# A state-space vision layer on one core: low part, third time step and two products moved by one unit in the scan loop

## Chip, cores and metric

One core of a Trainium2 chip. The metric is the device time of the whole kernel in microseconds (us), lower is better. The kernel before took 372.35 us (median of 3 runs, 372.12 to 372.91).

## What is computed

A patch embedding, a selective state-space block (Mamba) and a mixture of experts, on 16 images of 64 tokens (1024 tokens), all in float32:

```python
h = patches @ proj_w.T + proj_b + pos_emb                 # 1024 x 192
# state-space block on layernorm(h); I = 384 channels, N = 16 states per channel
hidden, gate = split(layernorm(h) @ in_proj_w.T)
hid = silu(causal_conv(hidden, conv_w) + conv_b)          # 4 taps
ts, Bm, Cm = split(hid @ x_proj_w.T)                      # 48, 16 and 16 wide
dt = softplus(ts @ dt_proj_w.T + dt_proj_b)               # last token's times alpha
state[t] = exp(A * dt[t]) * state[t-1] + dt[t] * Bm[t] * hid[t]
y[t] = sum over states of state[t] * Cm[t]
h = h + ((y + hid * D) * silu(gate)) @ out_proj_w.T
# experts: 8, the best 2 of each token, and a shared one
h = h + sum_e cw[e] * ffn_e(layernorm(h)) + ffn_shared(layernorm(h))
```

## The kernel before

The tokens go in two groups g of 8 images (512 tokens), the 384 channels in three chunks i of 128 (one channel per partition). A vector z = 3g + i is one chunk of one group. The 16 states in halves of 8 and the 4 token tiles of a group make 8 slices of a vector, so there are 48 units n of 128 x 1024 elements: 0 to 23 for group 0 and 24 to 47 for group 1. Unit 24 is the first of vector 3, the "second group's first vector".

For each unit:

- ScalarE writes exp(A dt) into `decays`, four units (one k = n // 4) at a time (`decays_of(k)`, line 861). It waits until the products of the buffer's last use are done (`cs_ok`), and for the end of the time step's product (`end_ok`).
- TensorE makes the inputs dt B hid in PSUM (`inputs(n)`, line 1757) from `diagB` (B on block diagonals) and `stacked_u` (the transposed dt hid, copied so that it multiplies `diagB`). The PSUM banks alternate, so inputs(n) waits for scan n-2.
- VectorE scans (`scanned(n)`, line 1208) in place over `decays`.
- GpSimd multiplies by C (`weighted(n)`, line 623). TensorE sums over the states by transposing matmuls (`summed(n-3)`, line 1803).

Each engine has its own queue, written out by hand as a loop over the 48 units with `if n == ...` places for the other work; within a queue nothing overtakes. What group 1 needs before unit 24 runs so, i being the chunk:

- ScalarE makes the linear step and its logarithm (lines 794 to 802), which lands in `dt[1]` and `u` (`lnp_ok`).
- VectorE's `time_step(1, i)` (line 1145): dt = max(dt, 0) + u, all in SBUF.
- GpSimd's `inputs_of(pool, 1, i)` (lines 632 and 634): the last token's dt times alpha, then u = dt hid (`u_ok`).
- TensorE's `u_transposes(3)` in unit 21 (line 1666), into a PSUM bank.
- ScalarE's `u_high_part(3)` (line 837): the bank rounded to the format of TensorE's fast float32 path.
- VectorE's `u_low_part(3)` (line 1197): the bank less the high part.
- TensorE's `u_copies(3, half)` in units 22 and 23 (lines 1697 and 1699), which wait for both parts; ScalarE's `u_stacked(3, half)` (line 853) copies them to `stacked_u`. The first stands between the two halves of `decays_of(6)`, which belongs to units 24 to 27.

VectorE also builds the 8 slices of `diagB` for group 1 (`diagonal(1, s)`, line 1113) behind scans 18 to 25, and `segment_starts` clears the first column of each segment (line 1214, 0.11 us) behind scan 22 among others. The vectors 4 and 5 take their low part in another way, on ScalarE (`u_low_copy`). Their transposes stand in units 25 and 34.

The places in VectorE's and GpSimd's loop that the change touches are these; behind each `if` the steps stand in the order of the code.

Of the kernel before, what the change touches and what calls it, by code (L numbers as in the profile page):

```python
# [59 lines left out]
def program(nc, xT_d, projT_d, projb_d, pos_d, inT_d, par_d, xpT_d, dtT_d, outT_d, gateT_d, w13T_d, w2T_d, out_d):  # L60
    ctx = ExitStack()
    with ctx:
# [539 lines left out]
        def inverse_deviation(pool, chain, n):  # L602

            pool.wait_ge(aggr_ok, n + 1)
            sl = slice(TPG * (n % G), TPG * (n % G) + TPG)
            chain(pool.tensor_scalar(veps[:, sl], mv[:, sl, 1], EPS, 1.0, ALU.add, ALU.mult))
            if n != 1:
                pool.tensor_tensor(rstd[:, sl], veps[:, sl], neghalf[:, :], ALU.pow).then_inc(rstd_ok, 1)
                return
            pool.tensor_scalar(less_mean[:, :], mv[:, sl, 0], -1.0, None, ALU.mult)  # L610
            chain(pool.tensor_tensor(rstd[:, sl], veps[:, sl], neghalf[:, :], ALU.pow))
            pool.tensor_tensor(less_mean[:, :], less_mean[:, :], rstd[:, sl], ALU.mult).then_inc(rstd_ok, 1)

        def weighted(pool, n):

            g, i, s = of_unit(n)
            pool.wait_ge(scan_ok, n + 1)
            if i == 0 and s % 2 == 0:
                pool.wait_ge(c_ld[s // 2], 16 * (g + 1))
            if n >= SLOTS:  # L620
                pool.wait_ge(nsum_mm, n - SLOTS + 1)
            k, t = n // TPG, n % TPG
            pool.tensor_tensor(states[:, n % SLOTS, :].rearrange("p (n b s) -> p n b s", n=NH, b=2),  # L623
                               decays[:, k % DBUF, t, :, :, :].rearrange("p b n s -> p n b s"),
                               c_all[:, s, :].rearrange("p (n b s) -> p n b s", n=NH, b=2),
                               ALU.mult).then_inc(cs_ok, 1)

        def inputs_of(eng, g, i):

            eng.wait_ge(dt_ok, IC * g + i + 1)  # L630
            end = dt[g][:, i, S - 1::S]
            eng.tensor_tensor(end, end, par[:, i, P_ALPHA:P_ALPHA + 1].to_broadcast([128, GB]), ALU.mult).then_inc(end_ok, 1)
            eng.wait_ge(end_ok, IC * g + i + 1)
            eng.tensor_tensor(u[:, i, :], dt[g][:, i, :], hid[g][:, i, :], ALU.mult).then_inc(u_ok, 1)

        @block.gpsimd
        def _(pool):
# [39 lines left out]
            def diagonal_of(s):  # L677
                h, t = s // TPG, s % TPG
                pool.tensor_tensor(
                    diagB[:, s, :, :, :],  # L680
                    on_diagonal[:, :].unsqueeze(1).unsqueeze(1).to_broadcast([128, BLOCKS, NH, BLOCK]),
                    b_copied[:, :, t, NH * h:NH * (h + 1)].unsqueeze(3).to_broadcast([128, BLOCKS, NH, BLOCK]),
                    ALU.mult).then_inc(diag_pool, 1)
# [4 lines left out]
            for n in range(UNITS):  # L688
                weighted(pool, n)
                if n < 2:  # L690
                    diagonal_of(BUILT_BY_POOL[2 + n])
                if n == 2:
                    inputs_of(pool, 0, 1)
                if n == 6:
                    inputs_of(pool, 0, 2)
                if n in (18, 21, 23):
                    inputs_of(pool, 1, (18, 21, 23).index(n))
                if n == 44:
                    inverse_deviation(pool, chain, G)

# [320 lines left out]
        def _(dve):  # L1021
# [7 lines left out]
            def statistics(t, added):  # L1029
                dve.wait_ge(added, t + 1)  # L1030
                dve.bn_stats(stats[:, t, :], h0[:, t, :])
# [60 lines left out]
            def scan_coefficients(g):  # L1092

                dve.wait_ge(xp_mm, g + 1)
                dve.tensor_copy(ssm[:, g, :], ps[0:XP, YBANK if g else 0, :]).then_inc(ssm_ok, 1)
# [11 lines left out]
            def diagonal(g, s):  # L1107

                dve.wait_ge(b_mm, g + 1)
                if g:  # L1110
                    dve.wait_ge(dbu_mm, 2 * SLICES + s + 1)
                h, t = s // TPG, s % TPG
                dve.tensor_tensor(
                    diagB[:, s, :, :, :],
                    copied_b(g)[:, :, t, NH * h:NH * (h + 1)].unsqueeze(3).to_broadcast([128, BLOCKS, NH, BLOCK]),
                    on_diagonal[:, :].unsqueeze(1).unsqueeze(1).to_broadcast([128, BLOCKS, NH, BLOCK]),
                    ALU.mult).then_inc(diag_dve, 1)
# [9 lines left out]
            def convolved(g, i):  # L1127
                dve.wait_ge(hidden_ok, IC * g + i + 1)
                chain(tap(g, i, 1))
                chain(tap(g, i, 2))  # L1130
                tap(g, i, 3).then_inc(conv_ok, 1)
# [10 lines left out]
            def time_step(g, i):  # L1142

                dve.wait_ge(lnp_ok, IC * g + i + 1)
                dve.scalar_tensor_tensor(dt[g][:, i, :], dt[g][:, i, :], 0.0, u[:, i, :],
                                         ALU.max, ALU.add).then_inc(dt_ok, 1)
# [23 lines left out]
            def first_low(half):  # L1170

                if half:
                    dve.wait_ge(u_high_ok, 1)
                else:
                    dve.wait_ge(half_high, 1)
                tokens = slice(HALF * half, HALF * (half + 1))
                dve.tensor_tensor(u_low[:, tokens], first_u(half), u_high[:, 0, tokens].bitcast(F32),
                                  ALU.subtract).then_inc(u_low_ok if half else half_low, 1)
# [7 lines left out]
            def rest_stacked():  # L1186

                dve.wait_ge(stack_mm, 2)
                dve.tensor_copy(half_stacked(0, 1),
                                ps[:, 5:7, :].rearrange("p b (j m) -> p (b j) m", j=2)).then_inc(stacked_ok, 2)  # L1190

            def u_low_part(z):

                dve.wait_ge(u_high_ok, z + 1)
                if z:
                    dve.wait_ge(stack_mm, 2 * z)
                dve.tensor_tensor(u_low[:, :], ps[:, u_bank(z), :], u_high[:, z % IC, :].bitcast(F32),
                                  ALU.subtract).then_inc(u_low_ok, 1)

            def scanned(n):  # L1200

                k, t = n // TPG, n % TPG
                dve.wait_ge(decay_ok, k + 2 if n >= 2 else 1)
                dve.wait_ge(dbu_mm, n + 1)
                if k >= DBUF and t == 0:
                    dve.wait_ge(starts_ok, k)
                both = decays[:, k % DBUF, t, :, :, :].rearrange("p b n s -> p (b n s)")
                dve.tensor_tensor_scan(both, both, unit_banks(n).rearrange("p b n -> p (b n)"), 0.0,  # L1208
                                       ALU.mult, ALU.add).then_inc(scan_ok, 1)
# [47 lines left out]
            for n in range(UNITS):  # L1257
                scanned(n)
                if n == 0:
                    first_low(1)  # L1260
                    diagonal(0, BUILT_BY_DVE[2])
                if n == 1:
                    rest_stacked()
                if n == 2:
                    time_step(0, 1)
                    diagonal(0, BUILT_BY_DVE[3])
                if n == 3:
                    convolved(1, 1)
                if n == 4:
                    u_low_part(1)  # L1270
                if n == 5:
                    convolved(1, 2)
                if n == 6:
                    time_step(0, 2)
                if n == 11:
                    u_low_part(2)
                    scan_coefficients(1)
                if n == 12:
                    b_split(1)
                if n == 20:  # L1280
                    u_low_part(3)
                if n in (17, 20, 21):
                    time_step(1, (17, 20, 21).index(n))
                if 18 <= n < 18 + SLICES:
                    diagonal(1, n - 18)
                if n == 41:
                    with_skip(IC)
                if n in (14, 28, 31, 45):
                    gated_sum((14, 28, 31, 45).index(n))
                if n in (39, 40, 41, 42):  # L1290
                    with_output(n - 39)
                if n in (40, 41, 42):
                    statistics(n - 40, h1_ok)
                if n == 43:
                    moments(0, h1_ok)
                if n % TPG == 2 and TPG < n < UNITS - TPG:
                    segment_starts(n // TPG - 1)
# [776 lines left out]
```

## Time and profile before

| | |
|---|---|
| median of 3 runs | 372.35 us (372.12 to 372.91) |
| profiled execution | 372.61 us, span 370.8 us, mean granted TensorE clock 0.972 |
| TensorE busy | 328.7 us (89%) |
| VectorE busy | 251.2 us (68%) |
| GpSimd busy | 204.9 us (55%) |
| ScalarE busy | 194.1 us (52%) |
| scans, VectorE, line 1208 | 48, 107.4 us in all |
| products by C, GpSimd, line 623 | 48, 113.9 us in all |
| chain that ended last | TensorE 58%, VectorE 18%, issue 10%, ScalarE 7% |

The scans run from 46.6 to 187.6 us of the span. The shares are of the whole span and mix stages: embedding and projections up to about 45 us, the scan stage, the router to about 226 us, then the loop over expert tiles. In the rows below the engines are called PE (TensorE), PEld (its weight loads), DVE (VectorE), ACT (ScalarE) and POOL (GpSimd). A releaser in brackets is what ended the idle time.

### The profile page before, as it was taken

To read this page: it belongs to the slowest core of one execution; us is meant where nothing else is said; L and a number is where in the kernel's file an instruction comes from. 1 tells how busy PE (TensorE), PEld (TensorE's weight loads), DVE (VectorE), ACT (ScalarE), POOL (GpSimd) and SP (SyncE) were. 2 spreads that over 40 slices of the span, in tenths; PEclk is the share of its full clock that TensorE was granted. 3 is DMA by queue.
4 is the path that set the end of the run, shared out by engine and by line. 5 is a ranking of instruction groups with operands and counts; after the bars stand their busy time and mean duration, and the time that the engine had idled before them with its cause. 6 is when DMAs were issued, how large, how long until landed. Compare 5 with 4: busy or idle time off the path is not lost.

```text
span 370.8 us, 6616 instructions
## 1 busy us (share of the span) xinstructions
PE 328.7 (89%) x2034; PEld 263.8 (71%) x2035; DVE 251.2 (68%) x475; ACT 194.1 (52%) x332; POOL 204.9 (55%) x162
## 2 busy tenths in 40 slices
PE   5799977989998788799788879899999999999990
PEld 5753855747875676588675568678888888888870
DVE  1455799979998999999998699883333333333330
ACT  1146895937995666676925757752222222222220
POOL 8110088695896999898866258600333333333342
PEclk9899899989999999999899989999999999999998
DMA  6990899200023320410999992232333222333222
GB/s 189 261 322 6 332 320 334 61 1 5 0 99 129 115 113 4 113 44 2 233 240 302 272 241 92 101 93 56 46 53 51 48 44 48 50 50 50 36 21 21
DMA packets 32776, 42.60 MB, mean 115 GB/s; under 512 B 3328, under 2 KB 28720, under 8 KB 31728
## 3 DMA queue, kind: packets, MB, share of 16 engines
q1 hardware_dynamic: 26752, 36.43, 33.9%
q0 software_dynamic: 4080, 4.39, 7.6%
q10 hardware_dynamic: 1920, 1.46, 1.7%
q8 instruction: 14, 0.23, 0.3%
q14 instruction: 10, 0.08, 0.1%
HBM read 28.29 MB, written 13.99 MB: 114 GB/s over the span
## 4 chain that ended last, share of the span: by engine, by line
PE 58%; DVE 18%; issue 10%; ACT 7%; DMA 4%; POOL 1%; SPq 1%; DVEq 0%; POOLq 0%; ACTq 0%
PE ps L1977 9%; DVE decays L1208 6%; PE ps L1803 6%; PE ps L1757 4%; PE ps L1935 4%; PE ps L1941 3%; PE ps L1940 3%; PE ps L1936 3%; PE ps L1937 3%; PE ps L1938 3%; DMA c_all<-in_xT 3%; PE ps L1967 3%; DVE w L424 3%; ACT decays L861 2%; PE ps L1566 2%
## 5 line engine op out<-in xcount | busy, mean ns | idle before, releaser
L623 POOL TENSOR_TENSOR states<-decays,c_all 128x1024 f32<-128x1024 f32 x48 | 113.9, 2401 | 18.1 <-DVE decays L1208 18.1
L1208 DVE TENSOR_TENSOR_SCAN decays<-decays,ps 128x1024 f32<-128x1024 f32 x48 | 107.4, 2262 | 4.6 <-PE ps L1757 4.0
L729 POOL DMA_INDIRECT out<-ysb,token_r x23 | 36.1, 1570 | 69.5 <-DVE ysb L1467 58.0
L861 ACT ACTIVATE decays<-dt,negA 128x504 f32<-128x504 f32 (+1 forms) x104 | 62.0, 675 | 8.1 <-POOL states L623 8.0
L981 ACT ACTIVATE sa<-ps 128x512 f32<-128x512 f32 x31 | 18.5, 598 | 87.6 <-PE ps L1941 85.5
L1803 PE MATMUL ps<-ident,states 128*128 128x128 f32 x384 | 54.1, 285 | 3.4 <-POOL states L623 1.9
L1977 PE MATMUL ps<-w,hT 128*128 (+1 forms) x248 | 46.3, 330 | 3.8 <-ACT hT L985 3.8
L1757 PE MATMUL ps<-diagB,stacked_u 64*128 64x128 f32 x384 | 38.1, 295 | 12.0 <-DVE decays L1208 10.4
L1803 PEld LDWEIGHTS ps<-ident,states 128*128 128x128 f32 x384 | 42.5, 144 | 7.6 <-POOL states L623 2.9
L1977 PEld LDWEIGHTS ps<-w,hT 128*128 128x128 f32 x248 | 42.0, 191 | 7.2 <-ACT hT L985 3.7
L1757 PEld LDWEIGHTS ps<-diagB,stacked_u 64*128 64x128 f32 x384 | 28.4, 188 | 25.4 <-DVE decays L1208 15.5
L1445 DVE TENSOR_TENSOR xs_low<-ps,xs_high 128x256 fp32r<-128x256 f32 x23 | 9.8, 425 | 52.5 <-ACT xs_high L976 52.5
L1935 PE MATMUL ps<-w,xs_high 128*128 (+1 forms) x62 | 30.7, 496 | 2.6 <-DVE xs_low L1445 2.5
L715 POOL DMA_INDIRECT rows_scratch<-xn,pos_i x16 | 18.8, 1173 | 15.0 <-DVE pos_i L1390 10.4
L724 POOL COPY token_r<-token 128x1 int32 (+1 forms) x23 | 17.3, 751 | 16.8 <-DMA out<-h 16.8
L1937 PE MATMUL ps<-w,xs_low 128*128 (+1 forms) x62 | 24.7, 398 | 0.0
L1936 PE MATMUL ps<-w,xs_high 128*128 (+1 forms) x62 | 24.7, 398 | 0.0
L1940 PE MATMUL ps<-w,xs_high 128*128 (+1 forms) x62 | 24.6, 397 | 0.0
L1941 PE MATMUL ps<-w,xs_low 128*128 (+1 forms) x62 | 24.4, 394 | 0.0
L1938 PE MATMUL ps<-w,xs_low 128*128 (+1 forms) x62 | 24.2, 391 | 0.0
L1454 DVE TENSOR_TENSOR hm<-ps,sa 128x512 f32<-128x512 f32 x31 | 21.2, 682 | 3.5 <-PE ps L1941 3.5
L985 ACT ACTIVATE hT<-ps 128x512 f32<-128x512 f32 x31 | 18.4, 592 | 4.1 <-PE ps L1967 4.1
(217 smaller groups left out, 595.1 us busy)
## 6 DMA issues: line engine op xcount, KB each, us to landing
rows_scratch<-zeros SPq DMA_DIRECT2D x16, 520.0 KB, 9.5
c_all<-c_scratch SPq DMA_DIRECT2D x8, 1024.0 KB, 4.7
w_raw<-in_w13T SPq DMA_DIRECT2D x9, 512.0 KB, 9.7
w_raw<-in_w13T SPq DMA_DIRECT2D x18, 256.0 KB, 9.6
w<-in_w2T SPq DMA_DIRECT2D x9, 384.0 KB, 3.2
xs<-rows_scratch SPq DMA_DIRECT2D x23, 130.0 KB
c_all<-in_xT SPq DMA_DIRECT2D x8, 256.0 KB, 9.1
out<-h SPq DMA_DIRECT2D x1, 576.0 KB, 3.3
```

The lines of the kernel that those rows point to most:

```text
L623: pool.tensor_tensor(states[:, n % SLOTS, :].rearrange("p (n b s) -> p n b s", n=NH, b=2), decays[:, k % DBUF, t, :, :, :].rearrange("p b ...
L729: pool.indirect_dma_start(out=out_d, out_offset=bass.IndirectOffsetOnAxis(ap=token_r[:, r:r + 1], axis=0), in_=ysb[:, r, :], in_offset=Non ...
L861: return act.activation(decays[:, k % DBUF, tiles[0]:tiles[1], :, n, 1:], dt[g][:, i, tokens].rearrange("p (a b s) -> p a b s", b=2, s=S)[ ...
L1208: dve.tensor_tensor_scan(both, both, unit_banks(n).rearrange("p b n -> p (b n)"), 0.0, ALU.mult, ALU.add).then_inc(scan_ok, 1)
L1757: last = pe.matmul(unit_banks(n)[:, q, :].rearrange("p (n j t) -> p j n t", n=NH, j=BLOCKS)[:, j, :, :], stacked[rows, (IC * g + i) % 2, j ...
L1803: last = pe.matmul(summed_banks(z)[:, 128 * t:128 * (t + 1)], states[:, n % SLOTS, 128 * c:128 * (c + 1)], ident[:, :], start=(s == 0 and ...
L1935: pe.matmul(o, high[:, 0, :], wh, start=True, stop=False)
L1936: pe.matmul(o, high[:, 0, :], wl, start=False, stop=False)
L1937: pe.matmul(o, low[:, 0, :], wh, start=False, stop=False)
L1940: pe.matmul(o, high[:, 1, :], ends, start=False, stop=False)
L1941: return pe.matmul(o, low[:, 1, :], ends, start=False, stop=True)
L1977: last = pe.matmul(ps[:, 6 + r, 0:D], hT[:, r, c, :], we[:, c * D:(c + 1) * D], start=(c == 0), stop=(c == HC - 1))
```

## The change

Three places in the loops move. On VectorE `u_low_part(3)` goes from behind scan 20 to behind scan 21, and `time_step(1, 2)` from behind scan 21 to behind scan 22. On GpSimd the products `inputs_of(pool, 1, 1)` and `inputs_of(pool, 1, 2)` go from behind `weighted(21)` and `weighted(23)` to behind `weighted(22)` and `weighted(24)`.

```diff
@@ GpSimd, loop over units
-                if n in (18, 21, 23):
-                    inputs_of(pool, 1, (18, 21, 23).index(n))
+                if n in (18, 22, 24):
+                    inputs_of(pool, 1, (18, 22, 24).index(n))
@@ VectorE, loop over units
-                if n == 20:
+                if n == 21:
                     u_low_part(3)
-                if n in (17, 20, 21):
-                    time_step(1, (17, 20, 21).index(n))
+                if n in (17, 20, 22):
+                    time_step(1, (17, 20, 22).index(n))
                 if 18 <= n < 18 + SLICES:
                     diagonal(1, n - 18)
```

Behind scan 20 the order was low part, time step (1,1), diagonal (1,2), and is now time step (1,1), diagonal (1,2). Behind scan 21 it was time step (1,2), diagonal (1,3), and is now low part, diagonal (1,3). Behind scan 22 it was diagonal (1,4) and the clearing of the starts, and is now time step (1,2), then these. The same instructions run as before.

## Rows read from the trace of the kernel before

**Rows 1.** Busy time by stretch: us, then each engine's busy (x instructions), clock, DMA.
```profile
134.00:190.00 56.00, 47.03 (x413) 40.35 (x412) 55.28 (x48) 36.57 (x57) 52.47 (x25) 0.97 0.33 85
```

**Rows 2.** Who VectorE waited for, 98 to 190 us: total us, times, longest.
```profile
DVE u_low L1197 <- ACT u_high L837: 1.8, 1, 1.8
DVE decays L1208 <- ACT decays L861: 0.6, 1, 0.6
```

**Rows 3.** Timeline of VectorE: start us, us, engine, line, operation, out<-in.
```profile
104.68 1.05 DVE L1145 SCALAR_TENSOR_TENSOR dt<-dt,u 128x512 f32<-128x512 f32 x1
...
111.23 2.27 DVE L1208 TENSOR_TENSOR_SCAN decays<-decays,ps 128x1024 f32<-128x1024 f32 x1
115.30 0.69 DVE L1197 TENSOR_TENSOR u_low<-ps,u_high 128x512 fp32r<-128x512 f32 x1 [1.79 <-ACT u_high L837]
115.91 1.18 DVE L1145 SCALAR_TENSOR_TENSOR dt<-dt,u 128x512 f32<-128x512 f32 x1
117.01 0.68 DVE L1113 TENSOR_TENSOR diagB<-ps,on_diagonal 128x512 fp32r<-128x512 f32 x1
117.61 2.27 DVE L1208 TENSOR_TENSOR_SCAN decays<-decays,ps 128x1024 f32<-128x1024 f32 x1
119.80 0.66 DVE L1145 SCALAR_TENSOR_TENSOR dt<-dt,u 128x512 f32<-128x512 f32 x1
120.39 0.68 DVE L1113 TENSOR_TENSOR diagB<-ps,on_diagonal 128x512 fp32r<-128x512 f32 x1
120.98 2.27 DVE L1208 TENSOR_TENSOR_SCAN decays<-decays,ps 128x1024 f32<-128x1024 f32 x1
123.18 0.66 DVE L1113 TENSOR_TENSOR diagB<-ps,on_diagonal 128x512 fp32r<-128x512 f32 x1
123.83 2.22 DVE L1208 TENSOR_TENSOR_SCAN decays<-decays,ps 128x1024 f32<-128x1024 f32 x1
...
126.56 2.27 DVE L1208 TENSOR_TENSOR_SCAN decays<-decays,ps 128x1024 f32<-128x1024 f32 x1
...
136.52 2.26 DVE L1208 TENSOR_TENSOR_SCAN decays<-decays,ps 128x1024 f32<-128x1024 f32 x1
```

**Rows 4.** Timeline of ScalarE: high part, then last halves of the decays.
```profile
114.67 0.60 ACT L837 ACTIVATE u_high<-ps 128x512 fp32r<-128x512 f32 x1 [1.99 <-PE ps L1666]
...
121.90 2.53 ACT L861 ACTIVATE decays<-dt,negA 128x504 f32<-128x504 f32 x4
...
131.87 2.52 ACT L861 ACTIVATE decays<-dt,negA 128x504 f32<-128x504 f32 x4
```

**Rows 5.** Timeline of TensorE: transposes, inputs of 22, first copy, inputs of 24.
```profile
114.03 0.60 PE L1666 MATMUL ps<-ident,u 128*128 128x128 f32 x4
...
117.40 0.98 PE L1757 MATMUL ps<-diagB,stacked_u 64*128 64x128 f32 x6
...
119.16 0.36 PE L1697 MATMUL ps<-u_high,spread_u 128*128 128x256 f32 x1
...
123.31 0.66 PE L1757 MATMUL ps<-diagB,stacked_u 64*128 64x128 f32 x8
```

**Rows 6.** Timeline of GpSimd: products of units 17, 19, 20, 21, (1,1) and 23.
```profile
105.14 2.82 POOL L623 TENSOR_TENSOR states<-decays,c_all 128x1024 f32<-128x1024 f32 x1
...
111.87 2.36 POOL L623 TENSOR_TENSOR states<-decays,c_all 128x1024 f32<-128x1024 f32 x1
...
114.19 2.34 POOL L623 TENSOR_TENSOR states<-decays,c_all 128x1024 f32<-128x1024 f32 x1
...
119.96 2.74 POOL L623 TENSOR_TENSOR states<-decays,c_all 128x1024 f32<-128x1024 f32 x1 [3.43 <-DVE decays L1208]
...
122.95 1.28 POOL L634 TENSOR_TENSOR u<-dt,hidden 128x512 f32<-128x512 f32 x1
...
126.50 2.36 POOL L623 TENSOR_TENSOR states<-decays,c_all 128x1024 f32<-128x1024 f32 x1
```

**Rows 7.** Timeline around 189 us: VectorE's normalization and GpSimd's last product.
```profile
188.90 2.48 DVE L1056 TENSOR_SCALAR xn<-h,mv,rstd 128x192 f32<-128x192 f32 x1
...
188.90 2.36 POOL L623 TENSOR_TENSOR states<-decays,c_all 128x1024 f32<-128x1024 f32 x1
```

**Rows 8.** Busy time by stretch, columns as in rows 1.
```profile
221.00:224.50 3.50, 3.50 (x13) 3.12 (x13) 3.34 (x10) 2.05 (x3) 2.62 (x3) 0.59 0.41 145
```

## The prediction

> **What bounds the kernel now.** I read the page first (shares, the 40 slices, the chain), then the busy time by stretch, then what VectorE waited for, then the instructions of each engine around scans 20 to 24. The page's chain says that the end is reached over TensorE, but that is an average over stages: it holds for the expert loop, from about 226 us. In the scan stage VectorE is the engine without holes: from 134 to 190 us it is busy 55.3 of 56 us, against 47.0 for TensorE and 52.5 for GpSimd [rows 1]. Between 98 and 190 us VectorE waited twice: once 0.6 us ahead of a scan, and once 1.8 us ahead of `u_low_part(3)`, on ScalarE's `u_high` copy [rows 2]. So whatever moves the scans earlier after that wait should move everything behind them, and this change goes for exactly that wait.
>
> In VectorE's timeline [rows 3] scan 20 runs 111.23 to 113.50. The next instruction, the low part, starts at 115.30. It waits for the copy at 114.67 to 115.27 [rows 4], which waits for the four transposes that TensorE issues in unit 21, at 114.03 [rows 5]. The time step `(1,1)` (115.91) and the diagonal (117.01) need nothing of that, but stand behind it in the queue; scan 21 starts at 117.61 though its inputs have long been ready.
>
> **The change, part by part.** Nothing is added or taken away: one subtraction of 0.69, one time step and two products (a small and a large instruction each) change place. No DMA is issued by any of them, and no queue of SP or ScalarE is touched. I walk VectorE's queue from scan 20 to scan 24, since from scan 24 on the order is the old one. An instruction is recorded to start 0.08 before the end of the scan ahead of it (119.80 against 117.61 + 2.27), so I take start-to-start distances [rows 3].
>
> *Low part behind scan 21.* The time step can start at 113.42. Its inputs, the logarithms of ScalarE, were there by about 113. What it costs is set by GpSimd. The same instruction took 0.66 at 119.80, but 1.05 at 104.68 and 1.18 at 115.91 [rows 3]. Both long ones end 0.56 to 0.59 behind the start or end of a GpSimd product: 105.73 against 105.14, and 117.09 against 114.19 + 2.34 = 116.53 [rows 6]. So it waits for the running GpSimd instruction and then takes 0.6. At 113.42 the product of unit 19 is running until 111.87 + 2.36 = 114.23 [rows 6], so the time step ends at 114.8. The diagonal follows at 114.72 and scan 21, 0.60 later, at 115.32. Before it was 117.61: 2.29 earlier, which is the 1.80 of waiting, plus 0.61 for the low part that left, less about 0.1 for the longer block.
> The Trainium skill (SBUF — State Buffer, Who interferes with whom) says that a VectorE instruction with two SBUF inputs and a GpSimd one that reads SBUF exclude each other for the whole instruction, and that issue order decides. By it the moved time step pays 0.8 of waiting; a price of 0.66, as in the row at 119.80, would put scan 21 at 114.6. The trace agrees with the blocking at 104.68 and 115.91.
>
> Scan 21 ends at 117.59; the low part comes at 117.51. Its source is ready since 115.27 [rows 4], 2.2 us of cover, so no wait. It costs 0.61, the diagonal 0.59: scan 22 at 118.71, before 120.98. TensorE has the inputs of unit 22 by 117.40 + 0.98 = 118.38 [rows 5], cover 0.3.
> Who waits for the low part: TensorE's copies of the vector, which started at 119.16 [rows 5] behind the transposed sums of unit 19. The low part is there at 118.2, so 0.96 of cover; beyond it each microsecond would move these copies, the inputs of 23 and 24 queued behind them, and the second half of ScalarE's decays for scans 24 to 27.
>
> *Third time step behind scan 22.* Scan 22 ends at 120.98. The time step now comes at 120.90 and costs 0.59, if GpSimd is idle as it was at 119.80; the product of unit 21 (start 117.67, 2.36) ends at 120.03, so it is. The diagonal and the memset add 0.65 (123.18 to 123.83): scan 23 at 122.14, ending 124.36. Then diagonal, 0.58: scan 24 at 124.86, before 126.56. **Sum: 2.29 at scan 21, less 0.61 for the low part that comes in behind it, plus 0.59 for the time step that left that place, less 0.59 for the same time step behind scan 22: 1.68, by the walk 1.70 us earlier.**
>
> *What else scan 24 needs.* Nothing of TensorE's and ScalarE's order up to there changes: the inputs of unit 24 start at 123.31 [rows 5] and end at 123.97, and the second half of the decays ends at 121.90 + 2.53 = 124.43 [rows 4]. Both are ready, the second by only 0.43. That is the ceiling: if the first time step were not blocked, VectorE would be 0.7 sooner, but the scan could not start before about 124.5, a gain of 2.05. Nearest bound on the other side for that term: a time step that waits a whole product, 2.4; that is a rival below.
>
> *The two products on GpSimd.* They cost 0.29 + 1.28 [rows 6], unchanged. Moved behind units 22 and 24, each lets one weighted product through first. In the new order: unit 20 ends at 117.05 (2.82 long, like the one at 105.14 that let a time step in), 21 at 120.03, 22 runs 121.06 to 123.80 (2.74, as the one at 119.96), product `(1,1)` to 125.33, unit 23 to 127.69, before 126.50 + 2.36 = 128.86 [rows 6]. So GpSimd gains 1.17, not 1.70. ScalarE's next decays start on that signal and ended at 131.87 + 2.52 = 134.39 [rows 4]; they now end at 133.2. The scan that needs them, 28, stood at 136.52 [rows 3] and would want 134.82: 1.6 of cover. Product `(1,1)` is done at 125.33 instead of 124.23, and its reader, the transposes of unit 25, comes up on TensorE at about 126.7: covered. Product `(1,2)` is read nine units later. So I cost the move of both at nothing.
>
> *Behind scan 24.* VectorE has no hole to 165 us and the 0.6 us one hangs on ScalarE's decays, which hang on scan 35 over TensorE; the weight loads start on signals of the scans. All of it moves as one. The expert loop is a fixed length behind it. So the 1.70 should reach the end: profiled execution 372.61 - 1.70 = 370.91. It stands 0.26 above the median of the runs, so for the median 372.35 - 1.70 = **370.65, called 370.7 us**.
>
> **The rivals.**
> A. *The block is longer* (slower). At 114.23 both the time step and the weighted product of unit 20 are waiting. At 105.14 VectorE went first. At 188.90 it was the other way: the normalization was recorded to start at 188.90 and took 2.48, with a GpSimd product starting at 188.90 [rows 7]. If GpSimd goes first at 114.23, the time step ends at 117.1 as before, scan 21 starts at 117.61 as before, and the low part behind it is pure delay: copies 1.3 us late, scan 24 at about 127.15, that is 0.6 slower: 372.95. It decides from the point where the time step reaches the block less than some 0.1 us before the product's end; it has 0.8, and had 0.46 at 104.68. Against it also: the Trainium skill's rule of issue order, same page and section, names the time step first (issued 113.42, the product of unit 20 after 113.5). The same at the second time step would cost 2.3 and leave 373.0; there it leads by 0.16 as at 119.80.
> B. *Capped by GpSimd and ScalarE.* If the cover of 1.6 on scan 28 is less than I think, or the 0.43 on scan 24, the gain is that of GpSimd, 1.17, or less: 371.2 to 371.6.
> C. *The clock.* From 221.0 to 224.5 TensorE's granted clock was 0.59 on average, mostly the lower level, 1.2 GHz, while it was busy throughout [rows 8]; it is one of five such stretches in the trace. If shorter gaps of TensorE around 115 and 125 us bring one more into the expert loop, it costs 3.5 x 0.41 = 1.4: 372.1. With A it would be 374.4.
> D. *More than the wait.* If at 188.90 the normalization wins its tie against the last product, up to 1.4 us of the chain goes as well, before TensorE's transposed sums become last: 369.3. Nothing makes this likelier than before.
> E. *It doesn't do what it says*, the wait coming back at the new place: 372.35. The source is ready 2.2 us ahead, so hardly.
>
> **How the numbers follow.** Forecast (370.3 to 371.1) 0.64; B 0.10; A 0.10; C 0.06; D 0.06; E or something unseen on either side 0.04. To keep 8 in 10 the range takes the forecast, B, C, D and leaves out A: 369.3 to 372.6. Measurement can tell about 0.2%, 0.74 us: faster is below 371.6, slower above 373.1. Faster: forecast, D and most of B, 0.78; within: A mostly, C, E, 0.17; slower: A with C or with its second place, 0.05.
>
> **What would show it.** VectorE's wait ahead of the low part is gone from the list of waits; time step `(1,1)` starts at about 113.4 and takes 1.3 to 1.4; scan 21 starts near 115.3, scan 24 near 124.9; TensorE's copies still start near 119.2; the inputs of 24 and the decays before scan 24 keep their times; scan 28 waits for nothing; all later instructions stand 1.7 earlier. The prediction is wrong if time step `(1,1)` takes 3.5 (A), if a wait on ScalarE's decays stands ahead of scan 24 or 28 (B), or if scan 24 is 1.7 earlier and the last instruction is not (C, D).

## Result and profile after

In the first comparison (20 runs of each kernel) the changed kernel took 370.0 us in the median (366.2 to 373.9), the one before 372.1 (367.8 to 373.9). The ratio is 0.9911 with a 95% interval of 0.9886 to 0.9937: 3.3 us faster, where 1.7 (0.9954) was forecast. One thing is needed to read that ratio: it leaves out runs more than 1.5% above the fastest of their kernel, which were 6 of 20 of the changed kernel (its fastest is lower) and 2 of 20 of the one before, so 1.3 of the 3.3 us comes from leaving them out: over all 20 the means differ by 2.0 us (369.99 against 371.99, standard error 0.6).

The profiled execution took 369.68 us. From its page:

```profile
span 367.9 us, 6616 instructions
PE 57%; DVE 17%; issue 9%; DMA 6%; ACT 6%; POOL 3%; SPq 1%; POOLq 0%; DVEq 0%; ACTq 0%
```

Who VectorE waited for between 98 and 190 us, as in [rows 2]: total, times, longest.

```profile
DVE decays L1208 <- ACT decays L861: 0.6, 1, 0.6
DVE h L1234 <- PE ps L1835: 0.5, 1, 0.5
```

The 1.8 us ahead of the low part are gone. The second line is new; it comes back below. VectorE's timeline from scan 20 on, the counterpart of [rows 3]:

```profile
108.97 2.27 DVE L1208 TENSOR_TENSOR_SCAN decays<-decays,ps 128x1024 f32<-128x1024 f32 x1
111.17 1.33 DVE L1145 SCALAR_TENSOR_TENSOR dt<-dt,u 128x512 f32<-128x512 f32 x1
112.42 0.68 DVE L1113 TENSOR_TENSOR diagB<-ps,on_diagonal 128x512 fp32r<-128x512 f32 x1
113.03 2.27 DVE L1208 TENSOR_TENSOR_SCAN decays<-decays,ps 128x1024 f32<-128x1024 f32 x1
115.22 0.66 DVE L1197 TENSOR_TENSOR u_low<-ps,u_high 128x512 fp32r<-128x512 f32 x1
...
116.40 2.27 DVE L1208 TENSOR_TENSOR_SCAN decays<-decays,ps 128x1024 f32<-128x1024 f32 x1
118.59 0.66 DVE L1145 SCALAR_TENSOR_TENSOR dt<-dt,u 128x512 f32<-128x512 f32 x1
...
119.85 2.22 DVE L1208 TENSOR_TENSOR_SCAN decays<-decays,ps 128x1024 f32<-128x1024 f32 x1
...
122.58 2.27 DVE L1208 TENSOR_TENSOR_SCAN decays<-decays,ps 128x1024 f32<-128x1024 f32 x1
...
132.54 2.25 DVE L1208 TENSOR_TENSOR_SCAN decays<-decays,ps 128x1024 f32<-128x1024 f32 x1
```

Two things are to be seen. Scan 20 already starts at 108.97, before it was 111.23: 2.26 us come from ahead of the change, where both kernels are the same. And from scan 20 to scan 24 it is 122.58 - 108.97 = 13.61 us, before 15.33: 1.72 us. The two must be kept apart, and that is the subject of the experiments. I therefore read every trace in four parts, by the starts of scans 20, 24 and 47 and the end of the span.

GpSimd (units 19, 20 and 22), ScalarE (high part, last halves of the decays for units 24 and 28) and TensorE (first of the copies), the counterparts of [rows 6], [rows 4] and [rows 5]:

```profile
109.60 2.36 POOL L623 TENSOR_TENSOR states<-decays,c_all 128x1024 f32<-128x1024 f32 x1
111.92 2.79 POOL L623 TENSOR_TENSOR states<-decays,c_all 128x1024 f32<-128x1024 f32 x1
...
118.75 2.75 POOL L623 TENSOR_TENSOR states<-decays,c_all 128x1024 f32<-128x1024 f32 x1 [0.99 <-DVE decays L1208]
```

```profile
112.39 0.60 ACT L837 ACTIVATE u_high<-ps 128x512 fp32r<-128x512 f32 x1 [2.00 <-PE ps L1666]
...
119.62 2.53 ACT L861 ACTIVATE decays<-dt,negA 128x504 f32<-128x504 f32 x4
...
128.37 2.52 ACT L861 ACTIVATE decays<-dt,negA 128x504 f32<-128x504 f32 x4
```

```profile
116.88 0.36 PE L1697 MATMUL ps<-u_high,spread_u 128*128 128x256 f32 x1
```

### The profile page after: what moved, and what is told of

Read it like the earlier page. It is cut to its first block, busy times and chain, and to the rows that moved or that the text cites. A ratio compares the mean times of both kernels' runs of the same rounds, so it can differ in the third digit from the quotient of the medians.

```text
span 367.9 us, 6616 instructions
## 1 busy us (share of the span) xinstructions
PE 329.8 (90%) x2034; PEld 264.5 (72%) x2035; DVE 251.2 (68%) x475; ACT 194.1 (53%) x332; POOL 204.7 (56%) x162
## 3 DMA queue, kind: packets, MB, share of 16 engines
q10 hardware_dynamic: 1920, 1.46, 1.6%
## 4 chain that ended last, share of the span: by engine, by line
PE 57%; DVE 17%; issue 9%; DMA 6%; ACT 6%; POOL 3%; SPq 1%; POOLq 0%; DVEq 0%; ACTq 0%
PE ps L1977 9%; DVE decays L1208 7%; PE ps L1803 6%; PE ps L1757 4%; PE ps L1935 4%; PE ps L1940 3%; PE ps L1936 3%; PE ps L1937 3%; PE ps L1941 3%; PE ps L1938 3%; DMA c_all<-in_xT 3%; DMA out<-ysb,token_r 3%; PE ps L1967 3%; ACT decays L861 3%; DVE w L424 2%
## 5 line engine op out<-in xcount | busy, mean ns | idle before, releaser
L1803 PEld LDWEIGHTS ps<-ident,states 128*128 128x128 f32 x384 | 43.3, 146 | 8.9 <-POOL states L623 4.2
L1757 PE MATMUL ps<-diagB,stacked_u 64*128 64x128 f32 x384 | 39.4, 300 | 9.5 <-DVE decays L1208 8.1
L1757 PEld LDWEIGHTS ps<-diagB,stacked_u 64*128 64x128 f32 x384 | 29.3, 192 | 23.5 <-DVE decays L1208 13.3
## 6 DMA issues: line engine op xcount, KB each, us to landing
w<-in_w2T SPq DMA_DIRECT2D x9, 384.0 KB, 13.6
```

The source lines that it names most:

```text
L1757: last = pe.matmul(unit_banks(n)[:, q, :].rearrange("p (n j t) -> p j n t", n=NH, j=BLOCKS)[:, j, :, :], stacked[rows, (IC * g + i) % 2, j ...
L1803: last = pe.matmul(summed_banks(z)[:, 128 * t:128 * (t + 1)], states[:, n % SLOTS, 128 * c:128 * (c + 1)], ident[:, :], start=(s == 0 and ...
```

## Experiments

Theory 1: the change is worth the 1.7 us of the walk (the sum along VectorE's queue in the prediction), and the rest of the 3.3 is TensorE's granted clock, which falls elsewhere in each execution. Theory 2: the change is worth 3 us, so something behind scan 24 gains too.

### The kernel before against itself, and the change again

No edit in the first, the whole change in the others.

> The kernel before, unchanged, timed against itself. It measures what this comparison makes of no change, and how the position of the stretches of low granted clock differs from one execution to the next. Theory 1 (the change is worth 1.7 us and what was measured beyond that is the clock): single times spread over 4 us or more with the mean granted clock, some 2.5 us of time for each 0.009 of clock, and the ratio can be off 1 by up to 0.5% without any change. Theory 2 (the change is worth 3.3 us): times of before stay within 1 us of 372.3 and the ratio within 0.2% of 1. Scan 20 to scan 24 takes 15.33 us in the profile wherever the low clock falls.

> The change as it is, timed again. Theory 1: in the profile scan 20 to scan 24 takes 13.6 us (15.33 before), and at equal mean granted clock the time is 1.7 us below before. Theory 2: at equal clock it is 3 us or more below.

> The change once more, to pool its single times. Theory 1: the mean over all runs is 1.7 us (1.2 to 2.3) below the mean over all runs of before; scan 20 to scan 24 is 13.61 us again. Theory 2: the mean stays 3 us below.

> The change once more. After three comparisons the mean of all its single times is 2.0 us below that of before (standard error 0.36), and the traces give 1.72 us from scan 20 to scan 24 and nothing elsewhere that is not a stretch of low clock. Theory 1: with these times added the mean difference lies between 1.3 and 2.3 us; in the profile the time from the start of scan 20 to the end of the span is 1.7 us below a trace of before that has its stretches of low clock in the same places behind scan 20. Theory 2 (the change also makes such stretches rarer or cheaper): the difference stays above 2.5 us.

What was timed (means are over all single times):

| comparison | kernel | runs | mean us | before: runs | mean us | ratio (95% interval) |
|---|---|---|---|---|---|---|
| first | change | 20 | 369.99 | 20 | 371.99 | 0.9911 (0.9886 to 0.9937) |
| n1 | before | 12 | 372.15 | 35 | 371.70 | 1.0038 (0.9999 to 1.0076) |
| n2 | change | 12 | 370.09 | the same 35 | 371.70 | 0.9962 (0.9925 to 1.0000) |
| n3 | change | 12 | 369.80 | 35 | 372.03 | 0.9906 (0.9868 to 0.9944) |
| n4 | change | 12 | 371.69 | 17 | 372.47 | 1.0001 (0.9964 to 1.0038) |

The same two kernels give ratios from 0.991 to 1.000, with intervals that shut each other out (n3 and n4), and the kernel before against itself is off by 0.4%. Single times of either span 6 us or more. Over all, 56 times of the change have a mean of 370.34 and 119 of before (the 12 of the null among them) one of 372.00: 1.66 us, with a standard error of 0.32 from their standard deviations (2.12 and 1.62). That fits the forecast of 1.70; that it agrees to 0.04 us is luck, given the error. The first comparison's 3.3 is well outside twice the error, its 2.0 over all single times is not. So no total here can confirm 1.7 against 1.2 or 2.2; the traces below do that.

The expectation of n2 also named the difference at equal mean granted clock: 1.7 us by theory 1, 3 or more by theory 2. Neither came. Single times do follow the clock: 0.01 less of it goes with 2.2 us more before (99 times, correlation -0.80) and 2.9 with the change (56 times, -0.90). One common slope for both kernels puts the change 2.5 us below before at equal clock (standard error 0.2; n2 and n3 2.8 and 2.9, n4 1.5). About 0.8 of that is given back, since the changed kernel's mean clock is lower by 0.0035 (standard error 0.0011), and 1.7 is left. Equal clock is no fair comparison, though: the mean counts the low clock at the very end of the span, which costs nothing, and in the traces below a long stretch of low clock between 55 and 64 us costs about as much up to scan 20 (108.3 and 109.0 us) as a short one between 74 and 78 (108.6). What the 2.5 consists of stays open.

The parts of the traces (us; the last column names the stretches, to 1 us, in which the mean granted clock was under 0.97; a short one is 3 to 4 us at the lower level, a long one about 7). In every trace the clock is low once more over the last 3 to 6 us of the span, where TensorE's work is done; the column leaves that out, as it costs nothing:

| trace | start to scan 20 | 20 to 24 | 24 to 47 | 47 to end | low clock at |
|---|---|---|---|---|---|
| before | 111.23 | 15.33 | 58.79 | 185.45 | 15-20, 39-43, 77-81, 182-187, 220-224 |
| before (n1) | 108.61 | 15.32 | 59.31 | 185.96 | 74-78, 149-153, 187-191, 217-222 |
| change | 108.97 | 13.61 | 59.31 | 186.01 | 55-63, 148-152, 185-189, 216-220 |
| change (n2) | 106.97 | 13.61 | 59.30 | 185.12 | 144-149, 175-183 |
| change (n3) | 111.37 | 13.61 | 59.31 | 186.41 | 36-44, 77-82, 149-153, 186-194, 221-225 |
| change (n4) | 108.33 | 13.61 | 60.66 | 187.30 | 56-64, 145-153, 186-190, 216-221 |

The column 20 to 24 is the same to 0.01 us in every trace of a kernel. All the others move, and in all of them the kernels are mixed. The part up to scan 20 is the widest, and all kernels of this document issue the same work there, so what it gives or takes does not come from the edits. Over all twelve traces it goes by the low clock in it: 106.9 and 107.0 us without a stretch (p3, n2), 108.3 and 108.6 with a short one (p2, n1), 108.3 to 109.2 with a long one (n4, p1, first of the change, p4), 111.2 to 111.7 with three short ones or a long and a short one (before, n3, p5), 113.9 with a long one and one twice as long (p6). Busy time by stretch of that part, columns as in [rows 1], the granted clock third from the end; first the trace of before, then n2 of the change:

```profile
35.00:50.00 15.00, 14.36 (x83) 10.48 (x83) 11.54 (x22) 12.40 (x30) 3.07 (x3) 0.89 0.79 276
...
70.00:85.00 15.00, 13.89 (x69) 7.78 (x67) 11.86 (x7) 8.63 (x14) 10.81 (x6) 0.89 0.01 2
```

```profile
35.00:50.00 15.00, 13.60 (x96) 10.20 (x94) 13.54 (x22) 14.21 (x33) 5.68 (x5) 1.00 0.86 302
...
70.00:85.00 15.00, 13.89 (x87) 8.19 (x86) 13.45 (x10) 10.31 (x18) 12.36 (x8) 1.00 0.00 1
```

In both stretches TensorE is busy, n2 gets more matmuls done in the same 15 us (96 against 83, 87 against 69), and the engines behind it do more as well. This ties the lost time to the low clock by where the two fall together; no run set the clock itself.

The cleanest pair is n1 of before and the first trace of the change: behind scan 20 their low clock lies in the same three places, to about 1.5 us. By the rows for 145 to 155 us, first n1, then the change:

```profile
145.00:155.00 10.00, 8.12 (x65) 6.79 (x63) 10.00 (x7) 5.64 (x10) 9.05 (x5) 0.83 0.34 105
```

```profile
145.00:155.00 10.00, 8.63 (x70) 7.54 (x71) 10.00 (x7) 6.64 (x11) 9.11 (x5) 0.83 0.36 105
```

Their page and scans 20 and 24 of n1:

```profile
span 369.2 us, 6616 instructions
108.61 2.27 DVE L1208 TENSOR_TENSOR_SCAN decays<-decays,ps 128x1024 f32<-128x1024 f32 x1
...
123.93 2.27 DVE L1208 TENSOR_TENSOR_SCAN decays<-decays,ps 128x1024 f32<-128x1024 f32 x1
```

From scan 20 to the end: 369.2 - 108.61 = 260.59 in n1, 367.9 - 108.97 = 258.93 with the change, 1.66 us less. So the gain at scan 24 reaches the end undiminished, and nothing is added to it. Two more pairs have their low clock behind scan 20 in the same places, to within 1 us. From scan 20 to the end the low part alone (p1) takes 261.13 and n3 259.33, 1.8 us apart with 1.83 up to scan 24. The products left in place (p4) take 259.48 and the first trace of the change 258.93, 0.55 apart with 0.59 up to scan 24.

Not all that moves is the clock. Behind scan 47 n4 has its low clock where the first trace of the change has it, to 1 us, and still takes 187.30 against 186.01. That 1.3 us arises at 236 us, with the clock at 1.00 from 226 to 240: ScalarE and TensorE stand still there, and the profile names no instruction of the core that they wait for. The second trace of the diagonal first has the same at 240 us; the other ten show no such wait. From n4:

```profile
236.06 0.60 ACT L985 ACTIVATE hT<-ps 128x512 f32<-128x512 f32 x1 [0.85 <-remote]
236.71 1.57 PE L1977 MATMUL ps<-w,hT 128*128 128x192 f32 x8 [1.12 <-issue]
```

The part 24 to 47 is 58.79 without a stretch of low clock between 144 and 153 us, 59.3 with one and 60.7 with two. The new wait of VectorE on L1835 belongs to it and not to the change: n1 of the kernel before has it too, and n2 of the change, with its stretch a few us earlier, has not. From the waits of n1:

```profile
DVE h L1234 <- PE ps L1835: 0.5, 1, 0.5
```

### The low part alone

```diff
-                if n == 20:
+                if n == 21:
                     u_low_part(3)
                 if n in (17, 20, 21):
                     time_step(1, (17, 20, 21).index(n))
```

> Only the low part goes behind scan 21; the time steps stay behind 17, 20, 21 and the products behind 18, 21, 23. Theory 1 with the block between VectorE and GpSimd: the third time step then stands behind the low part, some 0.5 us after GpSimd began the product of unit 21, and waits for its end: it takes about 2.5 us instead of 0.66, scan 22 starts 12.1 to 12.5 us after the start of scan 21's predecessor is over by 2.3, that is at the place it had before, and scan 20 to scan 24 takes 15.4 us: no gain at all (0.0 to +0.2 us). Rival, no block: the whole 1.7 us comes from the low part alone, scan 20 to 24 takes 13.6 us.

VectorE's scan 20, the third time step and scan 24; then GpSimd's product of unit 21:

```profile
108.77 2.27 DVE L1208 TENSOR_TENSOR_SCAN decays<-decays,ps 128x1024 f32<-128x1024 f32 x1
...
115.61 2.51 DVE L1145 SCALAR_TENSOR_TENSOR dt<-dt,u 128x512 f32<-128x512 f32 x1
...
124.21 2.27 DVE L1208 TENSOR_TENSOR_SCAN decays<-decays,ps 128x1024 f32<-128x1024 f32 x1
```

```profile
115.18 2.38 POOL L623 TENSOR_TENSOR states<-decays,c_all 128x1024 f32<-128x1024 f32 x1 [0.67 <-DVE decays L1208]
```

The time step was issued 0.43 us after the product began and took 2.51: until 118.12, which is 0.56 behind the product's end at 117.56. From scan 20 to 24 it is 15.44 us. The wait of 1.8 is gone here too, and nothing is won. Twelve times have a mean of 372.07. So the low part frees the time, but only together with the moved time step does any of it arrive. The rival of the expectation (no block, 13.6 us) is out.

### The time step and the products alone

```diff
-                if n in (18, 21, 23):
-                    inputs_of(pool, 1, (18, 21, 23).index(n))
+                if n in (18, 22, 24):
+                    inputs_of(pool, 1, (18, 22, 24).index(n))
...
-                if n in (17, 20, 21):
-                    time_step(1, (17, 20, 21).index(n))
+                if n in (17, 20, 22):
+                    time_step(1, (17, 20, 22).index(n))
```

> The low part stays behind scan 20; the third time step goes behind scan 22 and the products behind 22 and 24. Both theories: the wait of 1.8 us ahead of the low part stays; scan 22 starts 0.6 us earlier, scan 23 where it was: scan 20 to scan 24 takes 15.3 us, no change (-0.1 to +0.2 us). If it is faster by more, the products' place on GpSimd is worth something by itself, which I costed at nothing.

```profile
108.25 2.27 DVE L1208 TENSOR_TENSOR_SCAN decays<-decays,ps 128x1024 f32<-128x1024 f32 x1
112.29 0.69 DVE L1197 TENSOR_TENSOR u_low<-ps,u_high 128x512 fp32r<-128x512 f32 x1 [1.77 <-ACT u_high L837]
...
123.57 2.27 DVE L1208 TENSOR_TENSOR_SCAN decays<-decays,ps 128x1024 f32<-128x1024 f32 x1
```

15.32 us from scan 20 to 24, as before, with the wait in its old place; mean of twelve times 372.52.

### The products left where they were

The changed kernel, with GpSimd's loop as before:

```diff
-                if n in (18, 22, 24):
-                    inputs_of(pool, 1, (18, 22, 24).index(n))
+                if n in (18, 21, 23):
+                    inputs_of(pool, 1, (18, 21, 23).index(n))
```

> The changed kernel, but with the two products of GpSimd left behind units 21 and 23. I costed their move at nothing. By the block between VectorE and GpSimd the product (1,1) then runs from about 9.1 to 10.35 us after the start of scan 20 (20 is 0), and the third time step, issued at 9.67, waits for its end: it takes 1.25 us instead of 0.66 and scan 20 to scan 24 takes 14.2 us, a gain of 1.1 instead of 1.7 us. Rival (the move is worth nothing, as I priced it): 13.6 us.

VectorE's scan 20, third time step and scan 24; GpSimd's product (1,1):

```profile
109.22 2.27 DVE L1208 TENSOR_TENSOR_SCAN decays<-decays,ps 128x1024 f32<-128x1024 f32 x1
...
118.86 1.24 DVE L1145 SCALAR_TENSOR_TENSOR dt<-dt,u 128x512 f32<-128x512 f32 x1
...
123.42 2.27 DVE L1208 TENSOR_TENSOR_SCAN decays<-decays,ps 128x1024 f32<-128x1024 f32 x1
```

```profile
118.27 1.28 POOL L634 TENSOR_TENSOR u<-dt,hidden 128x512 f32<-128x512 f32 x1
```

14.20 us, as expected: the product ends at 119.55, the time step at 120.10. So the move of the products is worth 0.59 of the 1.72. The ten times (mean 372.38, standard error 0.65) are too few to show the 1.1 us that the trace leaves.

### The low part one scan later still

The changed kernel with

```diff
-                if n == 21:
+                if n == 22:
                     u_low_part(3)
```

> The changed kernel with the low part one scan later still, behind scan 22 (ahead of the third time step). It measures the cover of 0.96 us that I gave the low part ahead of TensorE's copies. My theory: scan 22 comes 0.6 earlier, the low part ends about 1.8 us behind the place where TensorE wants it, the copies, the inputs of 23 and 24 and the second half of the decays follow, scans 23 and 24 wait: scan 20 to scan 24 takes 14.6 to 14.8 us (13.61 with the change, 15.33 before), the kernel some 1.1 us slower than the change and 0.6 us faster than before. Rival (TensorE and ScalarE have more slack than I read): scan 20 to 24 stays at 13.6 us.

VectorE: scan 20, low part, time step, scan 24. Then the product of unit 22, TensorE's first copy, and the stretch behind it:

```profile
106.93 2.27 DVE L1208 TENSOR_TENSOR_SCAN decays<-decays,ps 128x1024 f32<-128x1024 f32 x1
...
116.38 0.67 DVE L1197 TENSOR_TENSOR u_low<-ps,u_high 128x512 fp32r<-128x512 f32 x1
116.96 2.49 DVE L1145 SCALAR_TENSOR_TENSOR dt<-dt,u 128x512 f32<-128x512 f32 x1
...
123.18 2.29 DVE L1208 TENSOR_TENSOR_SCAN decays<-decays,ps 128x1024 f32<-128x1024 f32 x1 [0.33 <-issue]
```

```profile
116.54 2.36 POOL L623 TENSOR_TENSOR states<-decays,c_all 128x1024 f32<-128x1024 f32 x1 [0.82 <-DVE decays L1208]
```

```profile
117.14 0.36 PE L1697 MATMUL ps<-u_high,spread_u 128*128 128x256 f32 x1 [2.06 <-issue]
```

```profile
118.50:122.00 3.50, 3.50 (x22) 3.38 (x21) 3.50 (x4) 3.40 (x6) 2.30 (x3) 0.53 0.30 122
```

A miss: 16.25 us from scan 20 to 24, where 14.7 was expected. TensorE did wait for the low part: its row names no releaser, but the copy starts 0.09 behind the low part's end at 117.05. Behind scan 20 the low part ends 3.21 us later than with the change (10.12 against 6.91) and the copy starts 2.30 later (10.21 against 7.91), so 0.9 of the 3.21 was covered, as read. But I had left out my own rule: behind the low part the time step meets the product of unit 22, begun 0.42 us earlier, and takes 2.49 instead of 0.66. That 1.8 us is most of the cost. In this trace the clock was also 0.53 on average from 118.5 to 122, right in the copies, and scan 24 waited 0.33 more. Ten times have a mean of 372.69 (standard error 0.81), which can't show the loss.

### The diagonal ahead of the time step

```diff
+                if n == 20:
+                    diagonal(1, 2)
                 if n in (17, 20, 22):
                     time_step(1, (17, 20, 22).index(n))
-                if 18 <= n < 18 + SLICES:
+                if n != 20 and 18 <= n < 18 + SLICES:
                     diagonal(1, n - 18)
```

> The changed kernel with the diagonal (1,2) ahead of the time step (1,1) behind scan 20: the diagonal reads PSUM and runs while GpSimd holds the time step up. The time step is then issued about 0.2 us before the product of unit 19 ends, instead of 0.8. If VectorE still goes first: the time step takes 0.8 us, scan 21 comes 0.6 us earlier (3.5 us after scan 20), scan 22 waits a little for TensorE's inputs of unit 22 and stands 0.25 us earlier, and scan 24 0.2 to 0.3 us earlier (13.3 to 13.4), near the ceiling that ScalarE's decays set. If GpSimd wins at this shorter lead (rival A of the prediction): the time step takes 3.1 us and scan 20 to 24 takes about 15.3 us.

> The diagonal ahead of the time step once more. Scan 20 to scan 24 was 13.43 us in the first profile, 0.18 less than with the change; I expect 13.43 again, and a mean of all its times within 0.7 us of that of the change, since 0.18 us is below what these times can tell.

VectorE from scan 20, with scans 22 and 24; GpSimd's product of unit 19:

```profile
111.65 2.27 DVE L1208 TENSOR_TENSOR_SCAN decays<-decays,ps 128x1024 f32<-128x1024 f32 x1
113.84 0.66 DVE L1113 TENSOR_TENSOR diagB<-ps,on_diagonal 128x512 fp32r<-128x512 f32 x1
114.42 0.76 DVE L1145 SCALAR_TENSOR_TENSOR dt<-dt,u 128x512 f32<-128x512 f32 x1
...
118.89 2.29 DVE L1208 TENSOR_TENSOR_SCAN decays<-decays,ps 128x1024 f32<-128x1024 f32 x1 [0.33 <-PE ps L1759]
...
125.08 2.28 DVE L1208 TENSOR_TENSOR_SCAN decays<-decays,ps 128x1024 f32<-128x1024 f32 x1
```

```profile
112.28 2.36 POOL L623 TENSOR_TENSOR states<-decays,c_all 128x1024 f32<-128x1024 f32 x1
```

13.43 us (13.44 in the second trace), 0.18 less than the change. The time step came 0.22 us before the product's end at 114.64 and still went ahead of the next one: it ended at 115.18. The scan behind it gains 0.6, of which TensorE's inputs of unit 22 take 0.33 back (L1759 is L1757 of the other kernels, two lines on). The times (mean 371.23 of 12 and 370.59 of 6, standard errors 0.60 and 1.46) can't tell it from the change, so by the traces it is the shortest of the orders tried, and whether the kernel's time is shorter is open.

## Why the prediction was right in its mechanism and off in what was first measured

**The walk.** It holds term by term. Scan 21 was forecast 2.29 earlier and came 2.32 earlier (4.06 against 6.38 behind scan 20), scan 22 2.27 and 2.32, scan 23 1.69 and 1.72, scan 24 1.70 and 1.72.

**The first time step.** Forecast 1.3 to 1.4, measured 1.33, so it ended at 112.50, 0.54 behind the end of the product of unit 19. It came 0.79 us before the end of that product, went ahead of the next one, and made that one 2.79 long. The Trainium skill's rule of the prediction (SBUF — State Buffer, Who interferes with whom), by which issue order decides, agrees with it, and with the six other traces that have this time step right behind scan 20 (1.34 or 1.35 us in each).

**The cover of the low part.** The high part was ready 2.2 us ahead, as read. The low part ended at 115.88 and the copies started at 116.88, 7.91 behind scan 20 where it was 7.93: 1.0 of cover, forecast 0.96. That TensorE needs it by then is shown by the 2.06 us of waiting one scan later.

**ScalarE's decays before scan 24.** They ended at 122.15, 0.43 before the scan, as forecast. With the diagonal first scan 24 came within 0.26 of the corresponding end (122.29 + 2.53 = 124.82, against 125.08).

**GpSimd's products, costed at nothing.** The sum was right, the attribution was not. My walk took GpSimd to be idle when the third time step came, and only the move makes it so. Undone alone, it costs 0.59 us. The rest of the step held: the decays for scan 28 ended at 130.89, scan 28 started at 132.54, 1.65 of cover where 1.6 was forecast.

**The way to the end.** Forecast undiminished, measured 1.66 from scan 20 to the end between two traces with their low clock in the same places, and 1.66 (standard error 0.32) between the means of all times. What did not hold is the sentence that the expert loop is a fixed length behind the scans: from scan 47 to the end it was 185.1 to 187.3 us in the table's six traces.

**Rival A** (GpSimd first, 0.6 slower) did not happen, and the point from which it would decide is lower than a lead of 0.22 us; no run came near the 0.1 us named for it. The tie of [rows 7] is there again in the trace after (the normalization takes 2.77 for two, as before). **Rival B** is out by the 0.43 and 1.65 of cover. **Rival D** did not happen in any of the twelve traces: the first normalization takes 2.45 to 2.49 in all of them.

**What failed** is the step on the numbers: rival C and the width. I took the stretches of low clock of one profiled execution as part of the kernel, priced only a sixth one, at 1.4 us and 0.06, and said that measurement can tell 0.2%. They are a term of every single time instead, and the kernel before against itself was off by 0.4%. From the table, the part up to scan 20 alone took between 107.0 and 111.4 us in six traces (113.9 in the second one of the diagonal first, which had low clock for most of 36 to 51 and 60 to 68), 24 to 47 between 58.8 and 60.7, and the rest between 185.1 and 187.3. Most of that is the low clock, 1.3 us of the last part something else. Three runs that agreed within 0.8 us hid that: 119 runs of the same kernel have a standard deviation of 1.6. Against a mechanism of 1.7 us that term, with the runs left out, can double a comparison of 20 runs, as in the first one, or wipe it out, as in n4. The Trainium skill (TensorE: Matmul & The Clock Gate, Part 1: The HAM clock gate) says that the gate leaves the clock at one of two levels, full or half, and that how much of a kernel runs at the lower one varies from run to run; the traces agree, with 1.00 from 355 to 360 us and 0.50 from 364 us on in the first trace of the change, and stretches in other places each time.

**What stays open**: how the change acts on such stretches. The mean granted clock of its 56 single runs is 0.968, that of 99 of before 0.972, a difference of three standard errors, so it has more low clock. That is the direction of rival C, at a mean price of some 0.8 us; against it stands a gain of 2.5 us at equal clock, more than the 1.7 of the walk. Together they give the 1.66 of all times, and no run separates them. Why a stretch begins where it does was not tried either, nor what ScalarE and TensorE wait for at 236 us of n4.

## What to carry to other kernels

Move a waiting instruction behind work that is ready, but then check each instruction that changes place for what the neighbouring engine does at its new time: here the same move was worth 1.72, 1.13 or -0.11 us depending on whether a time step met a GpSimd product. Read such a change between two fixed instructions of the trace (scan 20 to scan 24 agreed to 0.01 us), and trust a total only over many runs, with a null beside it. Before a median of three is taken as the kernel's time, compare two profiled executions of the same kernel part by part.

## What the runs showed that I had not expected

- A blocked VectorE instruction looks busy: the time step is recorded as 0.66, 0.76, 1.24, 1.33, 2.49 or 2.51 us, and each long one ends 0.5 to 0.6 us behind the end of GpSimd's instruction. No view of waits shows it.
- When both engines wait for the same release, VectorE went first with leads of 0.22, 0.46 and 0.79 us, though GpSimd's next product was ready too; the product behind it then took 2.79 to 2.82 instead of 2.36.
- Two traces of twelve lose 1.3 us behind scan 47 at the full clock, on waits that no view of the profile puts down to an instruction of the core.
- One kernel's single times lie between 367.4 and 376.3 us, and the kernel before against itself gave a ratio of 1.0038 (0.9999 to 1.0076).
